# Gated cross-attention and switch-head attention on one core: turning the scores in two row tiles, and weighting moved in front of the turning

## The reference

```python
def _L0_xattn_ref(v, k, q, mask, wq, bq, wk, bk, wv, bv, wo, bo):   # 16 heads of 16
    qh = _split_heads(q @ wq + bq)
    kh = _split_heads(k @ wk + bk)
    vh = _split_heads(v @ wv + bv)
    logits = jnp.einsum('bhqd,bhkd->bhqk', qh, kh) / jnp.sqrt(jnp.float32(D))
    logits = logits + mask * -1000000000.0
    attn = jax.nn.softmax(logits, axis=-1)
    out = jnp.einsum('bhqk,bhkd->bhqd', attn, vh)
    out = out.transpose(0, 2, 1, 3).reshape(q.shape[0], -1, E)
    return out @ wo + bo
...
x = x + jnp.tanh(g_xattn[0]) * _L0_xattn_ref(ctx_1024, ctx_1024, _layernorm(x, axis=-1), mask_1x1xSxS2_fk1, ...)
x = x + jnp.tanh(g_ffn[0]) * _L0_ffn_ref(_layernorm(x, axis=-1), L0_ffn_Wq, L0_ffn_Wk, L0_ffn_Wv, L0_ffn_Ws, L0_ffn_Wd, L0_ffn_Wo)
```

## Time and profile before

| | us |
|---|---|
| three timed executions, median (lowest to highest) | 1313.19 (1313.13 to 1314.36) |
| the profiled execution | 1312.56 |
| its span, first to last instruction | 1310.8 |
| TensorE busy (share of the span) | 1250.7 (95%) |
| TensorE's weight loads | 1019.3 (78%) |
| VectorE | 865.4 (66%) |
| ScalarE | 611.9 (47%) |
| GpSimd | 550.0 (42%) |

### The profile page before, as it was taken

How to read it: one execution, slowest core, us unless ns; L and a number is a source line. 1 busy time by engine, 2 the same in 40 slices (tenths; PEclk the granted TensorE clock), 3 DMA queues, 4 the chain that set the end, 5 groups by cost and what they waited for, 6 DMA issues and landing times. The chain is left out here.

```text
span 1310.8 us, 40356 instructions
## 1 busy us (share of the span) xinstructions
PE 1250.7 (95%) x15928; PEld 1019.3 (78%) x15928; DVE 865.4 (66%) x2455; ACT 611.9 (47%) x1353; POOL 550.0 (42%) x823
## 2 busy tenths in 40 slices
PE   5799999999999999999978999999999999999996
PEld 4577777777787787777656888888888888888885
DVE  2566766766766676676656677667767666776651
ACT  3456556556555655555423443344344344433431
POOL 3476676666666667667510221222122122212111
PEclk9999999999999999999989999999999999999996
DMA  8898897787778778777305666565656656665663
GB/s 230 189 201 187 190 204 167 168 177 165 161 174 174 161 166 181 155 167 166 78 19 114 147 139 153 133 142 139 158 138 141 142 146 144 131 157 133 142 146 83
DMA packets 262976, 200.21 MB, mean 153 GB/s; under 512 B 195907, under 2 KB 243845, under 8 KB 258693
## 3 DMA queue, kind: packets, MB, share of 16 engines
q1 hardware_dynamic: 262788, 197.64, 65.8%
HBM read 125.49 MB, written 72.11 MB: 151 GB/s over the span
## 5 line engine op out<-in xcount | busy, mean ns | idle before, releaser
L753 POOL TENSOR_SCALAR shifted<-raw,neg_max 112x375 f32<-112x375 f32 x512 | 303.6, 601 | 194.0 <-DVE neg_max L646 127.9
L646 DVE CUSTOM_DVE_ANT_0 raw<-bank_s,maskb 112x375 f32<-112x375 f32 x512 | 269.0, 545 | 115.9 <-issue 76.2
L565 ACT ACTIVATE probsT<-bank_t 128x448 f32<-128x448 f32 x384 | 181.0, 547 | 162.0 <-PE bank_t L382 162.0
L382 PE MATMUL bank_t<-ident,shifted 112*128 112x112 f32 x1536 | 170.4, 260 | 3.0 <-POOL shifted L753 3.0
L382 PEld LDWEIGHTS bank_t<-ident,shifted 112*128 112x128 f32 x1536 | 155.7, 141 | 22.0 <-POOL shifted L753 19.2
L373 PE MATMUL bank_s<-K_stack,Q_stack 128*112 128x375 bf16 x512 | 157.8, 335 | 11.8 <-DVE neg_max L646 7.9
L1316 DVE TENSOR_REDUCE max<-bank_s 112x4 f32<-112x448 f32 x128 | 78.8, 616 | 75.8 <-PE bank_s L1043 75.8
L1403 POOL TENSOR_TENSOR mix_bd<-pm_te,tok 128x448 f32<-128x448 f32 x32 | 30.5, 953 | 209.1 <-DMA pm_te<-pm_dram 209.1
L995 PE MATMUL bank_ab<-xnT,wq2T 128*128 128x224 f32 x512 | 110.6, 359 | 0.4 <-ACT xnT L1159 0.4
L995 PE MATMUL bank_ab<-xnT,wk2T 128*128 128x224 f32 x512 | 109.6, 357 | 1.1 <-ACT kT L1188 0.6
L1392 POOL TENSOR_SCALAR var_eps<-moments 112x1 f32<-112x1 f32 x32 | 7.1, 222 | 233.8 <-DVE moments L1265 233.8
(11 more groups left out here) (135 smaller groups left out, 2205.3 us busy)
## 6 DMA issues: line engine op xcount, KB each, us to landing
K_stack<-k_dram SPq DMA_DIRECT2D x64, 562.5 KB, 7.4
k_dram<-k_parts SPq DMA_DIRECT2D x32, 562.5 KB, 4.9
att_dram<-att_q SPq DMA_DIRECT2D x32, 511.0 KB, 4.1
att_th<-att_dram SPq DMA_DIRECT2D x32, 511.0 KB, 4.3
v_dram<-mv SPq DMA_DIRECT2D x32, 455.0 KB, 6.1
v<-v_dram SPq DMA_DIRECT2D x32, 455.0 KB, 4.0
K_stack<-k_dram SPq DMA_DIRECT2D x32, 375.0 KB, 9.3
Q_stack<-q_dram SPq DMA_DIRECT2D x64, 168.0 KB, 9.2
```

The costliest lines, as they stand in the source:

```text
L382: last = nc.tensor.transpose(bank_t[0:KP, k, j * S:(j + 1) * S], shifted[:, g % 2, j, k * KP:(k + 1) * KP], c.ident[0:S, 0:S])
L565: act.activation(probsT[:, g % 2, k, :], bank_t[0:KP, k, 0:G * S], ACT.Exp).then_inc(exp_done, 1)
L646: dve.tensor_tensor_reduce(raw[:, g % 2, j, :], bank_s[h % 2][0:S, 0:S2], c.maskb[:, :], -1.0, -LEAST, ALU.add, ALU.min, neg_max[:, g % 2, ...
L753: pool.tensor_scalar(shifted[:, g % 2, j, 0:S2], raw[:, g % 2, j, :], -1.0, neg_max[:, g % 2, j:j + 1], ALU.mult, ALU.add).then_inc(shift_ ...
```

## The change

The turning of a group now goes through TensorE as two row tiles, the first 64 queries (partitions 0 to 63) and the other 48 (64 to 111). A unit is one block of 128 keys of one head, 12 in a group. The loop issues unit u of the lower tile and unit u + 10 (modulo 12) of the upper one, so that the two tiles of a pair write different banks; `PLACES` says which units lie in which bank. Before the lower tile comes to bank 2, TensorE waits for the first two transpositions of the upper tile (`upper_done`). ScalarE's exponentials follow the places: four in a group (512, 480, 256 and 96 columns) in place of three of 448, and they start when the whole group is turned. A turn as a whole waits for the exponentials of the group before it, no longer bank by bank.

In TensorE's `body`, `weigh` of a group moves to right in front of the `turn` of the next; the weighting of group 2 moves into the next round, behind scores 0 and 1. Scores 4, 8 and 12 and `keys` move up accordingly. On ScalarE `ctx_copy` goes in front of the exponentials of group 3, `key_copy` in front of `heads_copy`, and `copy_x` in front of the exponentials of group 2. On VectorE `split_queries` moves from behind head 1 to behind head 3. GpSimd's and SyncE's orders are unchanged.

```diff
+    UNITS, LOW = KC * G, z.S - 48
+    PLACES = ((0, 8, 0, 0, 0), (0, 10, 1, 1, 0), (8, 12, 0, 2, 0), (10, 12, 1, 2, 4 * LOW))
+    HALVES = ((0, LOW), (LOW, z.S))
...
             def turn(b, g, first):
                 pe.wait_ge(shift_done, H * b + G * g + G)
-                for k in range(KC):
-                    if not (first and g == 0):
-                        pe.wait_ge(exp_done, KC * (NG * b + g - 1) + k + 1)
-                    for j in range(G):
-                        last = nc.tensor.transpose(bank_t[0:KP, k, j * S:(j + 1) * S],
-                                                   shifted[:, g % 2, j, k * KP:(k + 1) * KP], c.ident[0:S, 0:S])
-                    last.then_inc(turned, 1)
+                if not (first and g == 0):
+                    pe.wait_ge(exp_done, len(PLACES) * (NG * b + g))
+
+                def one(half, u):
+                    lo, hi = HALVES[half]
+                    (bank, column), = [(bank, column + (u - first_u) * (hi - lo)) for first_u, end, h, bank, column in PLACES
+                                       if h == half and first_u <= u < end]
+                    k, j = u // G, u % G
+                    return nc.tensor.transpose(bank_t[0:KP, bank, column:column + hi - lo], shifted[lo:hi, g % 2, j, k * KP:(k + 1) * KP], c.ident[lo:hi, lo:hi])
+
+                for u in range(UNITS):
+                    if u == 8:
+                        pe.wait_ge(upper_done, NG * b + g + 1)
+                    one(0, u)
+                    last = one(1, (u + UNITS - 2) % UNITS)
+                    if u == 1:
+                        last.then_inc(upper_done, 1)
+                last.then_inc(turned, 1)
...
@@ body of TensorE
                 S_(0, 1)
                 if back:
+                    weigh(b - 1, 1 - p, NG - 2, False)
                     turn(b - 1, NG - 1, False)
...
-                S_(3)
+                S_(3, 4)
+                if ahead:
+                    keys(b + 2, p, 0)
+                S_(5)
                 if back:
                     weigh(b - 1, 1 - p, NG - 1, False)
-                S_(4)
-                if ahead:
-                    keys(b + 2, p, 0)
-                S_(5)
                 turn(b, 0, first)
...
@@ exps of ScalarE
-                for k in range(KC):
-                    act.wait_ge(turned, KC * (NG * b + g) + k + 1)
-                    act.activation(probsT[:, g % 2, k, :], bank_t[0:KP, k, 0:G * S], ACT.Exp).then_inc(exp_done, 1)
+                act.wait_ge(turned, NG * b + g + 1)
+                for first_u, end, half, bank, column in PLACES:
+                    lo, hi = HALVES[half]
+                    act.activation(probsT[:, g % 2, first_u:end, lo:hi], bank_t[0:KP, bank, column:column + (end - first_u) * (hi - lo)].rearrange("p (u q) -> p u q", q=hi - lo),
+                                   ACT.Exp).then_inc(exp_done, 1)
...
@@ body of ScalarE
+                if ahead:
+                    ctx_copy(b + 2, p, False)
                 if not first:
                     exps(b - 1, NG - 1, False)
                 if ahead:
-                    ctx_copy(b + 2, p, False)
+                    key_copy(b + 2, p, i + 1, 0)
                 if not first:
                     heads_copy(b - 1, second)
-                if ahead:
-                    key_copy(b + 2, p, i + 1, 0)
...
@@ body of VectorE
-                score_max(b, first, 0, 1)
+                score_max(b, first, *range(4))
                 if not first and not last:
                     split_queries(b + 1)
-                score_max(b, first, *range(2, 7))
+                score_max(b, first, *range(4, 7))
```

More of the change, by code:

```diff
@@ L246, in cross @@
         turned, exp_done, pv_done = sem("turned"), sem("exp_done"), sem("pv_done")
+        upper_done = sem("upper_done")
         headsT_copied, heads_ready, recip_done, heads_done = sem("headsT_copied"), sem("heads_ready"), sem("recip_done"), sem("heads_done")
@@ L437, in body @@
                 S_(5)
+                if back:
+                    weigh(b - 1, 1 - p, NG - 1, False)
                 turn(b, 0, first)
@@ L441, in body @@
                     keys(b + 2, p, 1)
-                weigh(b, p, 0, first)
                 if back:
@@ L447, in body @@
                 S_(8)
+                weigh(b, p, 0, first)
                 turn(b, 1, False)
@@ L463, in body @@
                 S_(13)
-                turn(b, 2, False)
                 if ahead:
@@ L467, in body @@
                     turn_x(b + 2)
+                weigh(b, p, 1, False)
+                turn(b, 2, False)
                 S_(14, 15)
@@ L750, in shift @@
                     h = G * g + j
-                    free = [] if j or (first and g < 2) else [(turned, KC * (NG * b + g - 1))]
+                    free = [] if j or (first and g < 2) else [(turned, NG * b + g - 1)]
                     wait_all(pool, v_set, (scores_read, H * b + h + 1), *free)
```

16 lines of the change are left out of this document (6 added, 10 removed).

## The result

The changed kernel took 1334.16 us in the median of four runs (1328.61 to 1341.18), the kernel before 1313.16 beside it: ratio 1.0152, 95% interval 1.0127 to 1.0177. It is slower, by 1.5%. The forecast was 1309.4, with a range to 1324; the time lies outside it. The profiled execution took 1334.58 us, its span 1332.9.

A forecast was written before the change was run, and what follows sets the result against it. TensorE, busy nearly throughout, bounded the kernel; after the change a loop through memory would set the round. Rounds 1 to 29 -3.2, round 30 +1.0, round 0 -1.3, tail -0.3: together -3.8, giving 1309.4 us; range 1297 to 1324.

The forecast's parts named there:

- The loop through memory: Queries' split, store, reload and next score 0: forecast at 19.31 us, longer than TensorE's round, so it sets the round.
- the store: SyncE's store of the split queries: issued 5.17 us after score 0 (4.90 to 5.40), not 3.09.
- The rule against the tiles: Skill's weight-load time in the turn: 107 ns a pair, a turn of about 1.4 us, slower; forecast set it aside.
- The chain, 14.0: From issue of the queries' store to landing of their last load: 13.6 to 14.4 us, taken as 14.0.
- handover: Between the last query load's landing and the next score 0: 0.14 us.
- B: Rival, chance 0.15: other transfers stretch the chain; slower from some 14.2 on, with 14.7 a round of 20.0, 1330 us.
- The second form of rival B: Keys' store takes its share from the last query load, so the chain grows; part of B's chance of 0.15.
- The pair, 0.055: Two row-tile transpositions in TensorE's turn: 0.055 us if the moved side decides, 0.064 in proportion to the load.
- entry of 0.15: TensorE's change into the row-tile shape at the start of a turn: 0.15 us.
- the 18.9: TensorE's own round after the change, were memory not binding: 18.9 us, from 19.42.
- Round 30 and the tail, +1.0 and -0.3: Round 30 set by memory: 18.5 against 17.4, +1.0; round 31 and tail, shorter turns less unhidden exponentials: -0.3 us.
- Round 0, -1.3: First round loses its last weighting to round 1 and has three shorter turns: -1.3 us.

The follow-up runs named there:

- the second trace: The changed kernel run and profiled once more with no edit; 1333.43 us in one run.

## Why the prediction was wrong

*Right.* The loop through memory sets the round, the store comes at 5.2 to 5.3, keys start at 4.0, and undoing the split undoes the loss. The rule against the tiles was rightly put aside: 12 pairs in 0.89. Keys waited 0.44 for the copy of ctx where 0.75 was forecast, since the scores before them ended later.

The forecast had rounds 1 to 29 at 19.31; they took 19.95 in the mean, which is 18.5 us. Two steps failed there, the size of the chain and a term that the sum left out.

*The chain, 14.0, was mis-sized: 14.3.* The round was added up as store, chain and handover. Measured, it is 5.28 + 14.29 + 0.04 = 19.6, not 19.31. The 25 rounds without one of the longer stalls bear this out: they average 19.62, which is 0.31 over the forecast, times 29 = 9 us. "I take 14.0" was read from rounds with 2 us of slack. B's limit "from some 14.2 on the kernel is slower" was right; the chance of 0.15 was too low: both ends of "13.6 to 14.4" had been read with a free queue before score 0, and the forecast kept them for a round without one. What lengthens the chain is not shown. The second form of rival B (the keys' store takes its share from the last query load) fits, at half its size, and moving the keys' store took 0.13 and 0.29 off the median chain, but two traces of one kernel differ by 0.12.

*The sum had no term for stalls.* Rounds 3, 4, 23 and 24, which hold the stalls of 0.6 to 2 us and the half clock behind some of them, take 9.6 us more than four of the others. That is as much as the chain, and with the chain alone the time would have come out near 1318, within the range. With half of the queries loaded, where the loop did not bind, the same four rounds take 7.8 us more than four others. Of eleven traces with the full turn in tiles eight have a stall of 0.6 us or more between 60 and 620 us on the matmuls, up to 2.0 in those with a split after score 2 or 3; of five traces with the old turn none has. With 9 of 24 transpositions left out there was none, in one trace; as three of the eleven had none either, this alone would not show it. TensorE has more instructions with the denser turn, and the queue that brings instructions has more transfers of 16 KB, 59 between 60 and 640 us against 49 in the kernel before. The three long stalls stand beside such transfers (1.1 to 1.3 us each, at 102.22, 514.02 and 534.64), but with two in every round that says little. That it is the fetching of instructions is inferred, not measured: the cause of the stalls stays open.

*The pair, 0.055, was mis-sized: 0.062.* With an entry of 0.15 (the forecast's), 0.89 gives 0.062 a pair, the bound "in proportion to the load" (0.064). "112 columns showed no trace of the load" drew a rule from a row that could not show one. Kernels without the memory loop have TensorE at 19.19, 0.29 over the 18.9; three turns before which nothing waits give 0.24 of it. That did not move the time, since memory bound.

*Round 30 and the tail, +1.0 and -0.3, came to +2.0 and +3.8.* Round 30 was put at a store of 4.8 and a chain of 13.6; it had 5.16 and 14.18, and in the second trace 5.16 and 13.28, which gives 18.5 as forecast. One chain scatters by as much as this miss. In the tail, score 0 to score 14 of the last batch takes 15.9 instead of 13.3, with the half clock behind the wait of 3.33. From there to the projection it takes 9.5 instead of 8.0, where the last two weightings wait 1.18 and 1.64 for exponentials that nothing hides. But the wait is not the cause of a long tail in general: the kernel with the early split, without such a wait, lost 8 us behind score 0 of the last batch (677.2 against 669.2), with a mean clock of 0.57 from 650 to 670 us. What a kernel loses there to the lower clock was not forecast and is not settled here.

*Round 0, -1.3, came to +1.0*: score 0 of batch 0 itself is 0.8 later, and score 13 waits 0.99. The wait of that first score for its queries differs by 2 us between kernels, 3.2 to 5.2 in all traces but one, and in the second trace of the changed kernel this part came to -0.8, so most of this miss is scatter.

Sum, for the profiled execution: 18.5 of the 26 us between forecast and measurement lie in rounds 1 to 29, 1.0 in round 30, 4.1 behind it, 2.3 ahead. That all have one sign is in part chance.

## What to carry to other kernels

Before moving a producer later in a loop that runs through memory, work out that loop's length with the queue as it will stand after the change, not from rounds with slack: here 14.3 for 14.0. A loop with no slack passes every late landing on, and a long wait can be paid again at the half clock. When a change makes the instructions of the busiest engine denser, give stalls a term of their own, or at least widen the range for them; here they cost as much as the chain. Test parts of a change in pairs as well as alone: here two parts that cost 0.30 and 0.71 a round gave 0.23 together, and the third, a gain of 0.3% by itself, cost 1.9% on top of them. The best of these kernels are the changed one with the early split and the old one with the late split, both 0.3% to 0.4% under the kernel before.

## What the runs showed of the hardware

- Two row tiles of 64 and 48 rows: 24 transpositions and 15 take the same 0.96 us. The smaller tile is free beside the larger, which takes 0.062 us for each 128-column load if the entry into the tile shape costs 0.15 (an estimate from the earlier trace rows).
- A store of 168 KB issued behind 1.5 MB of loads on one queue lands after 9.0 us instead of 2.5.
- Halving the bytes of the queries' loads, with as many pieces, shortened the landing of the last from 10.1 to 9.2 us and the chain by 1.0.
- TensorE stalled 0.6 to 2 us without a releaser, and only with the denser turn (8 of 11 traces, against 0 of 5 with the old one). Three such stalls stood at the same places of the program in two traces of one kernel.
- The granted clock fell to 0.50 for some 7 us behind a stall of 1.86 and behind a wait of 3.33, but not behind a wait of 2.41 in the second trace of the same kernel.
